# Graph layer and mixture of experts on one core: four more places for transposed masks, masks made six to three tiles ahead, another order on GpSimd and in the set-up

## The reference

```python
mask = (adj > 0).astype(x.dtype)                     # z = layernorm(x)
agg  = mask @ z / maximum(sum(mask, 1), 1)
comb = concat([z @ W_self + b_self, agg @ W_nb + b_nb]) @ W_comb + b_comb
x1   = x + relu(comb)
logits = layernorm(x1) @ Wg + bg                     # 8 experts, the best 2 of them
out  = x1 + sum over the 2 of softmax weight * (gelu(n @ W1[e] + b1[e]) @ W2[e] + b2[e])
```

## Time and profile before

| what | us |
|---|---|
| median of 3 runs | 505.43 (501.82 to 507.48) |
| the profiled execution: span, first to last instruction | 521.0 |
| TensorE / VectorE / ScalarE / GpSimd busy in the span | 444.2 / 370.7 / 257.6 / 305.2 |
| set-up, to the first product of tile 0 | 78.3 |
| neighbour loop, to the last product of tile 31 | 256.5 |
| from there to the end | 186.2 |

### The profile page before, as it was taken

One profiled execution on the slowest core, in us unless ns is written; L12 is line 12 of the kernel. 1 busy time (PEld: TensorE's weight loads), 2 busy tenths in 40 slices (PEclk: granted clock), 3 DMA queues, 4 the chain that ended last, 5 costly groups with the idle time before them and its releaser, 6 DMA issues.

```text
span 521.0 us, 12708 instructions
## 1 busy us (share of the span) xinstructions
PE 444.2 (85%) x4162; PEld 380.2 (73%) x4162; DVE 370.7 (71%) x1056; ACT 257.6 (49%) x403; POOL 305.2 (59%) x346
## 2 busy tenths in 40 slices
PE   4599989999999999989799899745999999997720
PEld 3388878888888888768688688633887778876610
DVE  2889744858758888679587798662677777679982
ACT  2558660543634354344354342330677777776630
POOL 2679778244355766756567563676255556555570
PEclk9789999999999999989999899965799999999975
DMA  8999898599999999999999931964555555588665
GB/s 247 267 264 270 239 243 221 147 278 258 256 272 277 298 306 307 299 297 276 301 282 307 291 132 62 275 230 153 166 164 164 164 161 153 149 325 335 195 211 161
DMA packets 49167, 122.47 MB, mean 235 GB/s; under 512 B 11081, under 2 KB 20173, under 8 KB 48080
## 3 DMA queue, kind: packets, MB, share of 16 engines
q1 hardware_dynamic: 31632, 68.29, 47.2%
q0 software_dynamic: 16080, 50.49, 32.4%
q10 hardware_dynamic: 1392, 2.88, 1.9%
HBM read 96.52 MB, written 26.93 MB: 237 GB/s over the span
## 4 chain that ended last, share of the span: by engine, by line
PE 27%; DVE 21%; DMA 19%; issue 12%; ACT 6%; SPq 6%; POOL 5%; another core or an unknown queue 2%; DVEq 1%; ACTq 0%; POOLq 0%
DMA wst<-in_L_ffn_W_dram 11%; PE bank L1326 7%; PE bank L1346 7%; PE bank L1227 6%; SPq L440 5%; POOL stage L563 3%; DMA x_sb<-in_x_dram 2%; DMA stage<-in_adj_dram 2%; PE bank L1218 2%; PE bank L1219 2%; DMA stage<-in_adj_dram,gidx 2%; PE bank L1313 2%; DVE stage L1112 2%; DVE mask L820 2%
## 5 line engine op out<-in xcount | busy, mean ns | idle before, releaser
L1218 PE MATMUL bank<-z_flat,maskT 128*128 128x257 f16 x1024 | 231.6, 277 | 0.7 <-issue 0.4
L1219 PE MATMUL bank<-z_lo,maskT 128*128 128x256 f16 x1024 | 231.5, 276 | 0.0
L642 POOL DMA_INDIRECT pair_out<-rows,enum x78 | 79.6, 1021 | 66.9 <-DVE gate L1125 29.7
L563 POOL DMA_INDIRECT stage<-in_adj_dram,gidx x64 | 76.0, 1188 | 64.3 <-ACT mask L667 52.0
L1218 PEld LDWEIGHTS bank<-z_flat,maskT 128*128 128x128 fp8e4 x1024 | 101.4, 99 | 14.2 <-issue 0.5
L1219 PEld LDWEIGHTS bank<-z_lo,maskT 128*128 128x128 fp8e4 x1024 | 101.4, 99 | 13.0 <-issue 0.3
L574 POOL DMA_INDIRECT dispatched<-rows,slot x64 | 65.9, 1030 | 39.5 <-issue 20.2
L710 ACT ACTIVATE xh<-x_sb,nb,rs 128x256 f32<-128x256 f32 x32 | 19.2, 600 | 139.6 <-POOL nb L631 139.6
L667 ACT ACTIVATE mask<-stage,m 128x2048 fp8e4<-128x2048 int32 x32 | 64.0, 2001 | 15.2 <-DVE maskT L827 7.5
L1346 PE MATMUL bank<-w,stage 128*128 x468 | 60.7, 281 | 8.2 <-DVE stage L1112 4.3
L1326 PE MATMUL bank<-stage,w 128*128 128x256 f16 x468 | 61.4, 284 | 6.2 <-DVE stage L1098 4.4
(11 more groups left out here) (175 smaller groups left out, 586.0 us busy)
## 6 DMA issues: line engine op xcount, KB each, us to landing
stage<-in_adj_dram SPq DMA_DIRECT2D x256, 128.0 KB
stage<-dispatched SPq DMA_DIRECT2D x39, 260.0 KB
wst<-in_L_ffn_W_dram SPq DMA_DIRECT2D x16, 256.0 KB
z_lo<-pair_out SPq DMA_DIRECT2D x4, 1024.0 KB
dispatched<-pad SPq DMA_DIRECT2D x15, 260.0 KB
out_dram<-x_sb SPq DMA_DIRECT2D x28, 128.0 KB
maskT<-pair_out SPq DMA_DIRECT2D x3, 1024.0 KB, 8.5
x_sb<-in_x_dram ACTq DMA_DIRECT2D x6, 256.0 KB, 8.5
```

The source lines that it names most:

```text
L563: gp.indirect_dma_start(out=stage[:, s, b - 2, :], out_offset=None, in_=adj_q[:, :], in_offset=bass.IndirectOffsetOnAxis(ap=gidx[:, 0:1], ...
L642: gp.indirect_dma_start(out=yp_dram[:, :], out_offset=bass.IndirectOffsetOnAxis(ap=enum[:, a, s:s + 1], axis=0), in_=ysb[:, a, s, :], in_o ...
L1218: mm(acc[u % 2][:, 0:D + 1], a, z_hi[:, i, :], start=(i == 0), stop=False)
L1219: last = mm(acc[u % 2][:, 0:D], a, z_lo[:, i, :], start=False, stop=(i == NT - 1))
```

## The change

Experts 4 to 7 of `w12` serve as four more places for transposed masks (8 to 11 in KEPT) once the last self product of the set-up is made (s_sp), until their weights are split (wait in expert_hi). Six masks are made in the set-up as before (the last behind pair 13, not 12), and made_in gives what a step masks: tiles 6 and 7 in steps 0 and 1, then t + 5, t + 4 and t + 3. turned_in says what VectorE transposes: 4 and 5 in step 0, then what the step before masked, now behind the low half and ahead of X1. Expert weights are loaded by ScalarE's queue behind the split. GpSimd makes rs and nb ahead of the gathers, and six of its eight additions of the constant (self_and_const, L593) move from the set-up into steps 1, 4, ..., 16. The sums of the maxima come behind a whole tile. In the set-up 52 matmuls of the identity precede the weights' transpositions, the bias product is made ahead of the pairs, the bias columns are loaded by GpSimd, and transpositions of pairs 2 to 4 and statistics go later.

```diff
-emr, fms = bank[2][:, 0:3], bank[1][:, D:D + 3]
+emr, fms = bank[2][:, 0:3], bank[7][:, 0:3]
...
 mask32 = [mask[:, i].rearrange("p b j -> p (b j)").bitcast(U32).rearrange("p (b k w) -> p b k w", b=G, k=NG) for i in range(2)]
-maskT32 = [maskT[:, i].bitcast(U32).rearrange("p (k b w) -> p b k w", b=G, k=NG) for i in range(4)]
-maskT8 = [maskT[:, i].rearrange("p (k m e) -> p k m e", k=NG, e=B) for i in range(4)]
+def at(t, n=1):
+    return slice(t, t + n) if isinstance(t, int) else bass.ds(t, n)
+masksT = [maskT[:, i] for i in range(4)]
+masksT += [w12[:, at(e), :, :, :, :].rearrange("p o w q t n -> p (o w q t n)").bitcast(F8) for e in range(E)]
+maskT32 = [m.bitcast(U32).rearrange("p (k b w) -> p b k w", b=G, k=NG) for m in masksT]
+maskT8 = [m.rearrange("p (k m e) -> p k m e", k=NG, e=B) for m in masksT]
...
-def at(t, n=1):
-    return slice(t, t + n) if isinstance(t, int) else bass.ds(t, n)
...
+WARM = 52
...
+def zt_behind(i):
+    return [j for j in {0: (2, 3), 1: (4,), 2: (5, 6), 3: (7, 8)}.get(i, (i + AHEAD,)) if j < PAIRS]
...
-MASKS, HELD, MADE = (1, 3, 6, 8, 10, 12), 4, 2
+MASKS, HELD = (1, 3, 6, 8, 10, 13), 4
+def made_in(s):
+    for first, end, ahead in ((0, 2, len(MASKS)), (3, 8, 5), (9, 18, 4), (19, NT - 3, 3)):
+        if first <= s < end:
+            return s + ahead
+    return None
+def turned_in(s):
+    if s == 0:
+        return range(HELD, len(MASKS))
+    m = made_in(s - 1)
+    return () if m is None else (m,)
+KEPT = ([0, 1, 2, 3, 8, 9, 10, 11] * 3)[:20] + [9, 10, 11, 0, 1, 2, 3, 11, 0, 1, 2, 3]
+assert len(KEPT) == NT
+def kept_before(t):
+    return max((i for i in range(t) if KEPT[i] == KEPT[t]), default=None)
+def last_kept(k):
+    return max((i for i in range(NT) if KEPT[i] == 4 + k), default=None)
 STATS = {0: 4, 2: 5, 3: 6, 5: 7}
+CONSTS = (1, 4, 7, 10, 13, 16)
...
         load_x(sp, i, (0, 1))
-    for w, b_ in enumerate((b_self, b_nb)):
-        sp.dma_start(bcol[:, w, :], b_.rearrange("(t p) -> p t", p=P), allow_slow_non_contiguous=True).then_inc(s_bcol, 16)
...
-    def load_expert(k):
-        if k:
-            sp.wait_ge(s_el, 2 * k)
-        for w, m in enumerate((W1, W2)):
-            sp.dma_start(wst[:, w], m[k].rearrange("(t p) n -> p t n", p=P)).then_inc(s_ew, 16)
...
             sp.dma_start(bg_bc[:, :], bg.rearrange("(o n) -> o n", o=1).to_broadcast((P, E))).then_inc(s_bc, 16)
-        if t == len(MASKS):
-            load_expert(0)
-        if t >= B + HELD + 1 and t % B == 1:
-            load_expert((t - HELD - 1) // B)
-    load_expert(E - 1)
...
     gp.memset(mhalf[:, :], -0.5).then_inc(s_io, 1)
+    for w, b_ in enumerate((b_self, b_nb)):
+        pool.dma_start(bcol[:, w, :], b_.rearrange("(t p) -> p t", p=P), allow_slow_non_contiguous=True).then_inc(s_bcol, 16)
...
     pool.dma_start(b1c[:, :, :], b1.rearrange("e (t p) -> p e t", p=P), allow_slow_non_contiguous=True).then_inc(s_b12, 16)
+    gather(6)
     self_and_const(0)
-    gather(6)
+    gather(7)
     self_and_const(1)
-    self_and_const(2)
-    gather(7)
-    for k in range(3, NG):
-        self_and_const(k)
...
             powers_of_e(NG - 1)
-        if HELD <= s < NT - 2 - MADE:
-            gather(s + 2 + MADE)
...
             gp.tensor_scalar(nb2[:, t:t + 1], mv2[:, t % B, 0:1], rs[:, t:t + 1], -1.0, ALU.mult, ALU.mult).then_inc(s_nb2, 1)
-        for _ in range(1 if s < NT - 2 - MADE else 2):
+        m = made_in(s)
+        if m is not None and m + 2 < NT:
+            gather(m + 2)
+        if s in CONSTS:
+            self_and_const(2 + CONSTS.index(s))
+        for _ in range(1 if s < NT - B else 2):
...
+    def load_expert(k):
+        if k:
+            act.wait_ge(s_el, 2 * k)
+        for w, m in enumerate((W1, W2)):
+            act.dma_start(wst[:, w], m[k].rearrange("(t p) n -> p t n", p=P)).then_inc(s_ew, 16)
...
         sc.copy(wT[:, w].rearrange("p t n -> p (t n)"), wps[w][:, :]).then_inc(s_wtc, 1)
-    for k in range(OWN // B):
-        normalise(k)
-    for i in range(AHEAD - 1):
-        zt_hi(i)
+    normalise(0)
+    zt_hi(0)
+    zt_hi(1)
...
         sc.activation(wf[:, 0, w, :], fold[w][:, :], ACT.Copy, scale=scw[:, 0:1]).then_inc(s_wfh, 1)
-    zt_hi(AHEAD - 1)
+    normalise(1)
...
         sc.activation(rows_f[:, at(2 * i, 2), 0:D], pair(sps[i % 2]), ACT.Copy, scale=scw[:, 2:3]).then_inc(s_self, 1)
-        if i + AHEAD < PAIRS:
-            zt_hi(i + AHEAD)
+        for j in zt_behind(i):
+            zt_hi(j)
...
             masks(t, t, t)
+    load_expert(0)
...
             expert_hi(div(t, u, known, ESPLIT, B))
-        if HELD <= known < NT - MADE:
-            masks(t + MADE, u + MADE, known + MADE)
+        m = made_in(t)
+        if m is not None:
+            masks(m, m, m)
+        if t >= ESPLIT and (t - ESPLIT) % B == 0 and (t - ESPLIT) // B < E - 1:
+            load_expert((t - ESPLIT) // B + 1)
...
         act.wait_ge(s_es, k + 1)
+        if last_kept(k) is not None:
+            act.wait_ge(s_mm, last_kept(k) + 1)
...
         dve.wait_ge(s_mA, t + 1)
-        if known is None or known >= 4:
-            dve.wait_ge(s_mm, t - 3)
-        v.transpose(maskT32[u % 4], mask32[u % 2]).then_inc(s_T, 1)
+        before = kept_before(t)
+        if before is not None:
+            dve.wait_ge(s_mm, before + 1)
+        elif t >= HELD:
+            dve.wait_ge(s_sp, PAIRS)
+        v.transpose(maskT32[KEPT[t]], mask32[u % 2]).then_inc(s_T, 1)
...
+    def biases():
+        dve.wait_ge(s_bcol, 32)
+        for w in range(2):
+            for t in range(KT):
+                v.tensor_scalar(bbig[:, w, t, :], ones[:, :], bcol[:, w, t:t + 1], None, ALU.mult).then_inc(s_bb, 1)
     stats(0)
-    stats(1)
-    stats(2)
+    biases()
...
     v.tensor_reduce(fmx[:, 1:2], wg_f[:, :, :].rearrange("p t n -> p (t n)"), AX.X, ALU.max, apply_absolute_value=True).then_inc(s_fmx, 1)
+    stats(1)
...
     dve.wait_ge(s_scw, 3)
-    v.tensor_scalar(wg_s[:, 0], wg_f[:, :, :], scw[:, 1:2], None, ALU.mult).then_inc(s_wf, 1)
-    dve.wait_ge(s_wf, 1)
-    v.scalar_tensor_tensor(wg_s[:, 1], wg_f[:, :, :], scw[:, 1:2], wg_s[:, 0], ALU.mult, ALU.subtract).then_inc(s_wf, 1)
...
         v.scalar_tensor_tensor(wf[:, 1, t, :], fold[t][:, :], scw[:, 0:1], wf[:, 0, t, :], ALU.mult, ALU.subtract).then_inc(s_wf, 1)
+    stats(2)
+    v.tensor_scalar(wg_s[:, 0], wg_f[:, :, :], scw[:, 1:2], None, ALU.mult).then_inc(s_wf, 1)
+    dve.wait_ge(s_wf, KT + 1)
+    v.scalar_tensor_tensor(wg_s[:, 1], wg_f[:, :, :], scw[:, 1:2], wg_s[:, 0], ALU.mult, ALU.subtract).then_inc(s_wf, 1)
     dve.wait_ge(s_idt, 4)
-    for i in range(2, AHEAD):
-        zt_lo(i)
     stats(3)
-    def biases():
-        dve.wait_ge(s_bcol, 32)
-        for w in range(2):
-            for t in range(KT):
-                v.tensor_scalar(bbig[:, w, t, :], ones[:, :], bcol[:, w, t:t + 1], None, ALU.mult).then_inc(s_bb, 1)
...
                                ALU.mult, ALU.subtract).then_inc(s_ul, 1)
-        if i + AHEAD < PAIRS:
-            zt_lo(i + AHEAD)
+        for j in zt_behind(i):
+            zt_lo(j)
...
         if i == 7:
-            biases()
-        if i == 9:
...
     def main_step(t, u, known):
-        if HELD <= known < NT:
-            mask_transpose(t, u, known)
...
                             row16[:, at(i), 0:D].rearrange("p o d -> p (o d)"), ALU.subtract).then_inc(s_lo2, 1)
+        for m in turned_in(t):
+            mask_transpose(m, m, m)
...
             v.tensor_scalar(ve[:, at(j)], mv2[:, r, 1:2], EPS, XS ** -2, ALU.add, ALU.mult).then_inc(s_ve2, 1)
-        if HELD <= known < NT - MADE:
-            masks(t + MADE, u + MADE, known + MADE)
+        m = made_in(t)
+        if m is not None:
+            masks(m, m, m)
...
-    pe.wait_ge(s_idt, 1)
+    pe.wait_ge(s_idt, 2)
+    for _ in range(WARM):
+        mm(bank[6][:, 0:P], ident[:, :], ident[:, :], start=True, stop=True)
...
-    pe.wait_ge(s_wtc, 2)
-    fold_weights(0)
-    fold_weights(1)
-    for i in range(3):
-        z_transpose(i)
-    pe.wait_ge(s_fmx, 3)
-    pe.wait_ge(s_idt, 4)
-    mm(fms, ones[:, :], fmx[:, 0:3], start=True, stop=True).then_inc(s_fmr, 1)
-    for i in range(3, AHEAD):
-        z_transpose(i)
...
+    pe.wait_ge(s_wtc, 2)
+    fold_weights(0)
+    fold_weights(1)
+    z_transpose(0)
+    z_transpose(1)
+    pe.wait_ge(s_fmx, 3)
+    pe.wait_ge(s_idt, 4)
+    mm(fms, ones[:, :], fmx[:, 0:3], start=True, stop=True).then_inc(s_fmr, 1)
+    const_product()
...
                 pe.wait_ge(s_ul, i // 2 + 1)
-            a = maskT8[u % 4][:, i // B, :, i % B]
+            a = maskT8[KEPT[u]][:, i // B, :, i % B]
...
             neighbours(u, 0, known == 0)
+            neighbours(u, 1, known == 0).then_inc(s_mm, 1)
...
             mm(emr[:, 2:3], ones[:, :], b1m[:, k:k + 1], start=True, stop=True).then_inc(s_emr, 1)
-        if live(known, 0):
-            neighbours(u, 1, known == 0).then_inc(s_mm, 1)
...
-    pe.wait_ge(s_wf, KT + 2)
+    pe.wait_ge(s_wf, KT)
...
             last.then_inc(done, 1)
```

(7 more changed lines are left out.)

## The result

Over 17 executions of each kernel the changed kernel took 509.02 us (median; 505.94 to 513.90), the kernel before 504.23 (500.14 to 508.47): a ratio of 1.0105, 95% interval 1.0075 to 1.0135. It is slower by 4.8 us where the forecast said faster by 7.7. The ratios leave out executions that lie well above the fastest of their kernel.

What follows compares the result with a forecast made beforehand. DMA was taken to bound the neighbour loop. Last mask 303.3 - 8.9 - 0.9 - 2.0 = 291.5, plus 35.6 gives last product 327.1, 7.7 less than 334.8; 505.4 - 7.7 = 497.7 us, range 492 to 503 (8 in 10: 485 to 505).

Steps and rivals of the forecast that it cites:

- likeliest case: The forecast itself: neighbour loop bound by DMA, 7.7 us less, 497.7 us; chance 0.54.
- rival C: Neighbour loop: VectorE stands for tiles asked ahead, last mask no earlier, 4.1 us paid for the lead, 509.5 us; chance 0.10.
- part 1: Start of the neighbour loop: four more mask places close the DMA hole, all later tiles land 8.9 us earlier.
- Part 1, second half: Neighbour loop: ten waits added on tile counts cost nothing, as VectorE waits in the same step for a younger tile.
- Part 2: End of the neighbour loop: four tiles, not three, run behind the last mask, 35.6 us instead of 31.5; costs 4.1.
- Part 3: Before the last mask: one tile fewer dispatched, 0.9 us gained, bounds 0 and 2.
- Part 4: Set-up in another order: tile 0 starts 4.5 us earlier, uncounted; earlier masks shrink smaller DMA holes, 2.0 us gained.
- Part 5: Neighbour loop: weights on ScalarE's queue, gathers behind rs and nb; 10.8 us of waits vanish, gain 0 if DMA-bound.
- Part 6: Loop steps 1 to 16: six of GpSimd's constant additions may slow VectorE, bounds 0 and 11.8 us; taken as 0.
- Rival A: Neighbour loop: only waits held it, TensorE becomes the bound, last product 20.0 us earlier, 485.4 us; chance 0.20.
- Rival B: Neighbour loop: GpSimd's additions slow VectorE, half of 11.8 us lands on the path, 503.6 us; chance 0.10.
- D: Set-up ends so late that masks 6 and 7 come at the hole's end; half the gain goes, 502.5 us; chance 0.06.

Runs made afterwards that it cites:

- kernel 6: Changed kernel with tiles masked two ahead from tile 27 on, so the last mask lies in step 29; ratio 1.0036 to the kernel before.
- kernel 7: Changed kernel with tiles 6 to 31 all masked two ahead, as in the kernel before, the rest of the change kept; ratio 1.0055 to the kernel before.
- 5: The changed kernel run again with no edit, as a yardstick; ratio 1.0075 to the kernel before.
- 13: Changed kernel with the maxima of expert weights one step later, scales in the step of the split, small products one tile later; ratio 1.0429 to the kernel before.
- 14: As 18, with the maxima of expert weights taken one step later; ratio 1.0034 to the kernel before.
- 15: The kernel before with nothing but the maxima of expert weights taken a step later; ratio 1.0515 to the kernel before.
- 17: As 18, with the first expert's weights asked for earlier, behind the twelfth pair of the set-up; ratio 0.9950 to the kernel before.
- 18: Changed kernel with VectorE reading the accumulator first, small products mid-tile, masks four ahead from step 3, two at the end; ratio 0.9917 to the kernel before.
- kernel 3: Changed kernel with expert weights loaded by SyncE's queue again; ratio 1.0082 to the kernel before.
- kernel 16: Changed kernel with GpSimd's six additions of the constant in the loop cut to 8 of 256 columns; ratio 1.0139 to the kernel before.
- kernel 4: Changed kernel with all eight additions of the constant made ahead of the neighbour loop again; ratio 1.0216 to the kernel before.
- kernel 9: Changed kernel with the three small products for an expert's scales back between the two halves of a tile; ratio 1.0061 to the kernel before.
- 8: Changed kernel with VectorE's reading of the accumulator and its statistics ahead of the mask's transposition; ratio 0.9971 to the kernel before.
- 10: Changed kernel with VectorE's order: accumulator reading and statistics, then lower half of the row, then transposition; ratio 1.0058 to the kernel before.

## Why the prediction was wrong

Its likeliest case was wrong; rival C, at 0.10 and 509.5 us, comes nearest: the last mask came 1.7 us earlier (301.59, 303.33), under the 4.1 that C named as its point, with VectorE standing for tiles asked ahead and X1 behind them. That its number fits 509.02 is luck in part: its price was the fourth tile behind the last mask, and kernel 6 took that tile away without an earlier last product; and kernel 7, without any early mask, is still 0.5% slower than before.

**The step that failed is the first: "I take the DMA as the bound of the loop", and with it "all later tiles land that much earlier, since nothing else idles the engines" in part 1.** The waits of before speak against it: in the loop VectorE and ScalarE stood 0.9 us in all for adj's data, 13.2 at the very most. A share of 1.04 says that the DMA engines were busy, not that anyone waited for them. The 8.9 us of hole were measured rightly and did close. Tile 8 landed 8.5 us earlier (97.4 for 105.9) and tile 12 even 13.8 (128.2 for 142.0). But earlier data is no earlier product. TensorE had not waited for data in the hole; it waits for the reading of an accumulator, and that stands on VectorE behind whatever VectorE waits for. The masks were put in front of it, and once tiles came to be used 13 us later and step 8 masked none, the DMA engines stood again at 140 to 160. "Nothing else idles the engines" left out the change's own steps without a mask. Kernels 5 and 7 show the exchange, 11.4 us against 12.1. Whether the DMA engines are still the bound of the later tiles is not settled: over 60 to 300 us they moved 273 GB/s at a share of 1.00 in both kernels. The argument against C, "a queue that is never empty can't land the last tile as late", fell with that: it was empty again.

Step by step:
- Part 1, second half, the ten waits added on tile counts, "they cost nothing": no list of waits has one of them. The cost was in the masks' own waits for data, 2.16 and 3.41 us in steps 1 and 2, where no younger tile had been waited for before.
- Part 2, the lead: 35.6 us from the last mask to the last product predicted, 35.7 measured (337.32 - 301.59). The size was right, its meaning wrong: kernel 6 shortened it to 30.9 and the last product stayed. It tells where the mask stands, and counts as a price only if the last mask sets the end.
- Part 3, one dispatch fewer (-0.9): no run separates it.
- Part 4: the first pair started at 21.75, 2.6 earlier (3 predicted), the products ahead took 5.0 (5.7; the trace has 51 of the 52). The clock was 0.50 there all the same in this execution, and tile 0 started 0.7 later where 4.5 earlier was forecast. ScalarE's set-up mask of tile 4 stood 5.2 us for its gather, and the pairs behind it with it. The start of tile 0 counted nothing in the sum. What counted were the 2.0 for smaller holes in the set-up: from 20 to 78 us the share is 0.98 where before had 0.96, some 1.1 us.
- Part 5: "the 10.8 of waits should vanish" is wrong; 10.0 stayed. "Two steps (15 us) between issue and use" was right and not enough: the transfer took 18.55 us beside full queues, 15.89 before. Its "0" for the loop was wrong in the other direction: each such wait holds a reading. What it is worth alone is not shown; of the four kernels meant to remove it three brought a larger wait (13, 14, 15), and one (17) did no better than its twin without the edit (18). The rule of the Trainium skill quoted there, several issuers save only issue time, agrees with kernel 3: on SyncE's queue or ScalarE's, ratio 1.0082 against 1.0075 to 1.0105, on different chips.
- Part 6: nothing speaks against the 0 in the time (kernel 16, without a yardstick on its chip). What I had not listed is that moving the additions was needed at all: left ahead of the loop they cost another 1% or more (kernel 4 against 3, same chip, intervals just apart; 3 differs from the changed kernel by its queue).
- Rival A (TensorE becomes the bound) did not come: 7.82 a tile behind the eighth, 7.4 being its own pace. Rival B's mechanism is in the trace (2.86) and has no price. D has not happened: masks 6 and 7 were made at 81 to 92, inside the old hole; its 502.5 was not half of the 7.7 either, which gives 501.6.

What stays open: where the 4.8 us by which the medians differ lie, as no trace of before on the same kind of chip exists; which part of the 0.5% of kernel 7 belongs to the small products and which to the rest; kernel 9 moved them back without a gain in the other setting. Why kernels 8 and 10 differ. And how much of the 21 us by which the loop stays behind TensorE's own pace (258.3 from first to last product, 32 tiles of 7.4 are 237) is due to DMA and how much to the steps: kernels that had the first eight tiles done anywhere from 134.5 to 149.5 ended their last product at 330.4 to 338.5 (kernel 4, which had them at 156.1, and kernels 9, 10, 13, 15 and 16 at 338.6 to 357.1), so something paces the rest at 8 us a tile, and no run separated its two candidates.

## What to carry to other kernels

A hole in the share of the DMA engines is worth what the engine at the end of the chain waits for during it: look first whether TensorE stood there at all, and whether anyone stood for data in the rest of the loop. Work that is pulled forward brings its waits with it; on an engine that works in order, put it behind the step on which the bound engine depends, and check the steps before the first such step too. Price a transfer's latency by the state of the queues after the change, not before it, and a stall of TensorE with the clock that follows it.
